# A different order of jobs on TensorE and of steps on VectorE in a fused attention and feed-forward kernel

## What is computed

```
xn = _layernorm(x)
q, k, v = split(xn @ Wqkv + bqkv)
qp, kp = elu(q) + 1, elu(k) + 1
kv = einsum('bsd,bse->bde', kp, v)                 # one sum over the 2048 rows of a batch
attn = (qp @ kv) / (qp @ sum(kp) + 1e-6)
z = layer_norm(xn + attn, g1, b1)
ffn = (silu(z @ Wg + bg) * (z @ Wu + bu)) @ Wd + bd     # Wg and Wu have 682 columns
s = layer_norm(z + ffn, g2, b2)
out = x + s * silu(xn @ (ternary(weight) * scale).T)
```

## Time and profile before

| what | value |
|---|---|
| median of 3 runs | 1211.54 us (1210.9 to 1212.32) |
| the profiled execution | 1212.66 us |
| its span in the profile | 1211.0 us |
| busy: TensorE matmul | 1190.9 us, 98% |
| busy: VectorE | 1082.2 us, 89% |
| busy: ScalarE | 953.3 us, 79% |
| busy: GpSimd | 841.7 us, 70% |

### The profile page before, as it was taken

The page is one execution under the profiler, slowest core; times in us unless marked ns, Lnnn a source line. Parts: engine busy times, 40 slices in busy tenths (PEclk is TensorE's granted clock), DMA queues, the critical chain, the costliest instruction groups (busy, mean ns, idle before and its releaser), DMA issues.

```text
span 1211.0 us, 24021 instructions
## 1 busy us (share of the span) xinstructions
PE 1190.9 (98%) x7550; PEld 1070.2 (88%) x7550; DVE 1082.2 (89%) x2467; ACT 953.3 (79%) x1557; POOL 841.7 (70%) x994
## 2 busy tenths in 40 slices
PE   8999999999999999999999999999999999999997
PEld 6889998989988999989999988999988899888886
DVE  6988999999999999999999999999999999777765
ACT  7787888878888887888878888778797788867753
POOL 3443787767787776787767777667776677766676
PEclk9999999999999999999999999999999999999999
DMA  7213432334432334432234432234332343222201
GB/s 217 74 50 88 123 106 70 88 105 123 123 104 72 87 106 123 118 103 78 87 106 122 121 104 74 74 120 123 108 96 63 101 123 105 70 71 61 76 22 35
DMA packets 137524, 115.61 MB, mean 95 GB/s; under 512 B 12340, under 2 KB 122294, under 8 KB 137399
## 3 DMA queue, kind: packets, MB, share of 16 engines
q1 hardware_dynamic: 137398, 114.08, 32.2%
HBM read 67.38 MB, written 46.67 MB: 94 GB/s over the span
## 4 chain that ended last, share of the span: by engine, by line
PE 86%; DVE 7%; issue 2%; ACT 2%; DMA 1%; POOL 1%; SPq 0%; DVEq 0%; POOLq 0%; ACTq 0%
PE bank L1271 61%; PE d_bank L1271 17%; PE xk_bank L1271 7%; DVE st L922 1%; DMA z_turned<-xa 1%; DMA xa<-z_turned 1%; DVE rz L1054 1%; PE bank L1285 1%; DVE bank L1095 0%; DVE h_l L1105 0%; ACT rz L695 0%; DVE zT_l L1085 0%; POOL norm L569 0%; ACT hs L695 0%; DVE kp L1014 0%
## 5 line engine op out<-in xcount | busy, mean ns | idle before, releaser
L1271 PE MATMUL bank<-zT_h,wgu_h 128*128 128x512 f32 x704 | 275.6, 391 | 1.1 <-DVE rz L1054 1.0
L1271 PE MATMUL bank<-zT_l,wgu_h 128*128 128x512 f32 x704 | 275.7, 392 | 0.0
L1271 PE MATMUL bank<-zT_h,wgu_l 128*128 128x512 f32 x704 | 275.4, 391 | 0.0
L695 ACT ACTIVATE rz<-rz,norm 128x256 f32<-128x256 f32 x252 | 140.5, 596 | 57.7 <-DVE norm L1131 57.1
L569 POOL TENSOR_TENSOR norm<-ve,consts 128x4 f32<-128x4 f32 x64 | 72.9, 1139 | 153.6 <-DVE ve L933 153.5
L1271 PE MATMUL d_bank<-wd_h,h_h 128*128 128x256 f32 x640 | 179.2, 280 | 0.1
L1271 PE MATMUL d_bank<-wd_h,h_l 128*128 128x256 f32 x640 | 179.0, 280 | 0.0
L1271 PE MATMUL d_bank<-wd_l,h_h 128*128 128x256 f32 x640 | 179.0, 280 | 0.0
L1095 DVE SCALAR_TENSOR_TENSOR bank<-bank,hb,hs 128x512 f32<-128x512 f32 x160 | 117.9, 754 | 54.0 <-ACT hs L695 42.3
L695 ACT ACTIVATE h_h<-bank 128x512 fp32r<-128x512 f32 x160 | 95.8, 599 | 80.9 <-DVE bank L1095 80.5
L1271 PEld LDWEIGHTS bank<-zT_l,wgu_h 128*128 128x128 f32 x704 | 132.1, 188 | 28.8
(11 more groups left out here) (163 smaller groups left out, 3576.3 us busy)
## 6 DMA issues: line engine op xcount, KB each, us to landing
xq<-in_L_attn_x_dram SPq DMA_DIRECT2D x32, 512.0 KB, 6.0
xa<-in_L_attn_x_dram SPq DMA_DIRECT2D x31, 512.0 KB, 3.9
out_dram<-rz SPq DMA_DIRECT2D x31, 512.0 KB, 5.0
z_turned<-xa SPq DMA_DIRECT2D x120, 128.0 KB, 3.3
xa<-z_turned SPq DMA_DIRECT2D x30, 512.0 KB, 4.1
turned<-xa SPq DMA_DIRECT2D x108, 128.0 KB, 2.5
xa<-turned SPq DMA_DIRECT2D x27, 512.0 KB, 3.9
rz<-in_L_attn_Wg_dram SPq DMA_DIRECT2D x1, 640.0 KB, 5.2
```

The lines of the kernel that those rows point to most:

```text
L695: return eng.activation(out_, in_, func, **kw).then_inc(S[name], 1)
L1271: ins = eng.matmul(dst, left, right, start=first and n == 0, stop=last and n == len(pairs) - 1, **kw)
```

## The change

Three things move. On TensorE, D 4 goes ahead of K 0, and XK 1 and XK 2 go ahead of U 4 (XK 0 stood there already, and XK 3 stays between U 4 and the last gate-up job). On VectorE, `zT_low` 1 goes ahead of `k_add` 0, `k_low` 1 ahead of `q_elu` 1 and `q_low` 0, and `h_low` 4 ahead of `x_low` 1. And the aggregation that ended `a_stats` becomes a step of its own, `a_aggregate`, which in the steady list stands behind `h_low` 1. No instruction is added or removed, and ScalarE, GpSimd and SyncE keep their order.

```diff
 TENSOR_JOBS = steps("""
-    K 0, D 4, KV 0, KV 1, D 5, K 1, N 0, N 1, N 2, N 3, G 0, U 0, G 1, U 1, G 2, B 0, U 2, Q 0, Q 1,
-    B 1, G 3, D 0, D 1, U 3, G 4, XK 0, U 4, XK 1, XK 2, XK 3, GU 5, D 2, TZ 0, TZ 1, D 3""")
+    D 4, K 0, KV 0, KV 1, D 5, K 1, N 0, N 1, N 2, N 3, G 0, U 0, G 1, U 1, G 2, B 0, U 2, Q 0, Q 1,
+    B 1, G 3, D 0, D 1, U 3, G 4, XK 0, XK 1, XK 2, U 4, XK 3, GU 5, D 2, TZ 0, TZ 1, D 3""")
...
 VECTOR_STEPS = steps("""
-    xk_low 0, zT_low 0, k_add 0, zT_low 1, kv_bias 0, kv_bias 1, kv_low 0, kv_low 1, ffn_rows 0,
+    xk_low 0, zT_low 0, zT_low 1, k_add 0, kv_bias 0, kv_bias 1, kv_low 0, kv_low 1, ffn_rows 0,
...
-    h_low 0, h_rows 1, a_stats 0, h_low 1, q_aggregate 0, h_rows 2, a_norm 0, x_turn 0, attn_norm 0,
...
+    h_low 0, h_rows 1, a_stats 0, h_low 1, a_aggregate 0, q_aggregate 0, h_rows 2, a_norm 0, x_turn 0, attn_norm 0,
...
@@ -956,7 +956,6 @@
                 for t in range(TILES):
                     stats(0, g, t, xa[:, g % 2, t, :])
-                aggregate(0, g)
```

More of the change, by code:

```diff
@@ L99 @@
 VECTOR_STEPS = steps("""
-    xk_low 0, zT_low 0, k_add 0, zT_low 1, kv_bias 0, kv_bias 1, kv_low 0, kv_low 1, ffn_rows 0,
+    xk_low 0, zT_low 0, zT_low 1, k_add 0, kv_bias 0, kv_bias 1, kv_low 0, kv_low 1, ffn_rows 0,
     ffn_rows 1, k_add 1, last_stats 0, attn 0, last_shift 0, attn 1, attn 2, attn 3, h_rows 0, k_max 0,
-    h_low 0, h_rows 1, a_stats 0, h_low 1, q_aggregate 0, h_rows 2, a_norm 0, x_turn 0, attn_norm 0,
-    k_max 1, h_low 2, k_low 0, q_elu 0, z_turn 0, q_elu 1, q_low 0, k_low 1, h_rows 3, h_rows 4,
-    q_low 1, h_low 3, x_low 0, h_rows 5, x_low 1, h_low 4, h_low 5""")
+    h_low 0, h_rows 1, a_stats 0, h_low 1, a_aggregate 0, q_aggregate 0, h_rows 2, a_norm 0, x_turn 0, attn_norm 0,
+    k_max 1, h_low 2, k_low 0, q_elu 0, z_turn 0, k_low 1, q_elu 1, q_low 0, h_rows 3, h_rows 4,
+    q_low 1, h_low 3, x_low 0, h_rows 5, h_low 4, x_low 1, h_low 5""")
 GPSIMD_STEPS = steps("""
@@ L145 @@
 FILL_VECTOR = fill("""
-    a_stats 0 0, a_stats 0 1, a_norm 0 0, a_norm 0 1, setup_k_low 0 0, xT_low 0 0, a_stats 1 0,
+    a_stats 0 0, a_stats 0 1, a_norm 0 0, a_norm 0 1, setup_k_low 0 0, xT_low 0 0, a_stats 1 0, a_aggregate 1 0,
     a_norm 1 0, setup_bk 0 0, xT_low 0 1, k_add 0 0, setup_q_low 0 0, xT_low 1 0, k_add 0 1, k_max 0 0,
-    a_stats 2 0, setup_bq 0 0, k_max 0 1, k_add 1 0, a_norm 2 0, xT_low 1 1, q_elu 0 0, k_max 1 0,
-    q_low 0 0, k_add 1 1, setup_gu_low_0 0 0, xT_low 2 0, k_max 1 1, a_stats 3 0, k_add 2 0, xT_low 2 1,
-    a_norm 3 0, setup_gu_low_1 0 0, q_elu 0 1, k_max 2 0, xT_low 3 0, k_add 2 1, a_stats 4 0, k_max 2 1,
+    a_stats 2 0, a_aggregate 2 0, setup_bq 0 0, k_max 0 1, k_add 1 0, a_norm 2 0, xT_low 1 1, q_elu 0 0, k_max 1 0,
+    q_low 0 0, k_add 1 1, setup_gu_low_0 0 0, xT_low 2 0, k_max 1 1, a_stats 3 0, a_aggregate 3 0, k_add 2 0, xT_low 2 1,
+    a_norm 3 0, setup_gu_low_1 0 0, q_elu 0 1, k_max 2 0, xT_low 3 0, k_add 2 1, a_stats 4 0, a_aggregate 4 0, k_max 2 1,
     setup_v_low 0 0, k_add 3 0, q_low 0 1, xT_low 3 1, a_norm 4 0, setup_d_bias 0 0, k_max 3 0,
-    k_add 3 1, a_stats 5 0, k_max 3 1, xT_low 4 0, setup_ternary 0 0, q_elu 1 0, xk_low 0 0, xT_low 4 1,
+    k_add 3 1, a_stats 5 0, a_aggregate 5 0, k_max 3 1, xT_low 4 0, setup_ternary 0 0, q_elu 1 0, xk_low 0 0, xT_low 4 1,
     k_add 4 0, kv_bias 0 0, kv_bias 0 1, a_norm 5 0, kv_low 0 0, kv_low 0 1, x_turn 5 0, k_max 4 0,
@@ L1260, in _ @@
                     "h_rows": (f, h_rows), "attn": (q, attn), "h_low": (f, h_low), "a_norm": (a + 1, a_norm), "x_turn": (a + 1, x_turn), "x_low": (a + 1, x_low),
-                    "q_aggregate": (q, lambda g, _: aggregate(1, g)), "last_stats": (last, last_stats),
+                    "a_aggregate": (a + 1, lambda g, _: aggregate(0, g)), "q_aggregate": (q, lambda g, _: aggregate(1, g)), "last_stats": (last, last_stats),
                     "attn_norm": (q, attn_norm), "z_turn": (q, z_turn), "last_shift": (last, last_shift),
```

## The result

The changed kernel takes 1228.34 us (median of 4 runs, 1228.14 to 1228.53) where the kernel before takes 1211.81 us beside it (4 runs, 1210.9 to 1212.32). The ratio is 1.0138 (95% interval 1.0123 to 1.0152): 16.5 us slower, past the upper end of the range. The profiled execution has a span of 1226.4 us, 15.4 more than before.

What follows compares the result with a forecast made beforehand. TensorE, 98% busy, was taken as the bound, so only waits counted: -1.8 + 4.8 + 2.0 = +5.0 us on the profiled 1212.66, or 1217.7, giving a median of 1216.5 us. The 8-in-10 range was 1209.5 to 1221.5 us.

Steps and rivals of the forecast that it cites:

- What bounds the kernel: TensorE, busy 98% of the span, sets the time; no matmul goes, so only its waits can be won or lost.
- A late handover costs x + 0.11 us: A TensorE job that waits x loses another 0.11 us, as its first weight load was not done ahead.
- Part one: Aggregation behind `h_low` 1: the 13 waits at Q 1 go, 0.14 us each, a gain of 1.8 us.
- Part two: `zT_low` 1 ahead of `k_add` 0 stands for GpSimd's `xn_low`; VectorE is 0.60 us later, costing 4.8 us at U 0.
- U 0's term: U 0 waits for the late `attn` 0 in 20 iterations, 0.24 us each: 4.8 us, bounds 2.8 to 6.6.
- What is late next: VectorE's remaining 0.36 us delay meets G 4 after `q_elu` 0: 0.1 us in 20 iterations, 2.0 us, bounds 0 to 9.4.
- Part three: XK 1 and XK 2 ahead of U 4, `k_low` 1 ahead of `q_elu` 1: room stays near 0.8 us, cost nothing.
- the third: VectorE's whole 0.60 us returns as waits at U 0, then G 4, XK 2 or U 4: 1225.7 us, chance 0.10.
- The first rival: VectorE keeps the port, does both `zT_low` in a row, GpSimd's `xn_low` behind them: 1209.0 us, chance 0.13.
- The second rival: `xn_low` may get the port first, so the delay stays under U 0's room: 1209.7 us, chance 0.15.
- the forecast's own range: 1212.5 us (2.8 at U 0, nothing at G 4) to 1222 (6.6 at U 0, half the bound at G 4).
- the signs named: `zT_low` 1 about 1.8 us, U 0's matmuls 0.34 apart, 20 more `rz` waits, Q 1's gone, iterations 36.0 to 36.2 us.

Runs made afterwards that it cites:

- f1: p1 with the shift step of `a_norm` moved behind `x_turn`: 1.0035 of the kernel before.
- p1: Kernel before with only the aggregation moved behind `h_low` 1: 1.0065 of the kernel before, +7.9 us.
- u2_aggregate: Changed kernel with the aggregation put back ahead of `h_low` 1: 1.0083 of the kernel before.
- e1: Kernel before with D 0 put ahead of Q 1 on TensorE, VectorE untouched: 0.9995 of the kernel before.
- p2_ztlow: Kernel before with only `zT_low` 1 moved ahead of `k_add` 0: 1.0079 of the kernel before, +9.2 us.
- m1_xnlow: Changed kernel with GpSimd's first `xn_low` moved behind the power `last_rstd`: 1.0176 of the kernel before, 1232.9 us.
- u3_both: Changed kernel with `k_add` 0 back between the two `zT_low` and the aggregation back ahead of `h_low` 1: 1.0003 of the kernel before.
- p3_xk: Kernel before with only XK 1 and XK 2 ahead of U 4, `k_low` 1 ahead of `q_elu` 1 and `q_low` 0: 1.0021, +2.6 us.
- p4_d4: Kernel before with only D 4 ahead of K 0 and `h_low` 4 ahead of `x_low` 1: 1.0014, +1.7 us.

## Why the prediction was wrong

**What bounds the kernel.** Right for the kernel before, and read too narrowly. I took TensorE's waits for the only thing to watch, and the engines around it for something with room. The chain after has 21% of TensorE and 79% of the rest: a delay of VectorE that is larger than the room of a handover isn't caught up there, but is met again further on. Which way around the engines holds the time is not shown. The way through SyncE's transfers and ScalarE's `zT_high` is one, but in f1 `zT_high` was on time and VectorE as late as in p1.

**A late handover costs x + 0.11 us.** Right: 0.06 us from release to start and 0.34 us to the second matmul, at U 0 as in the earlier trace rows.

**Part one, "the gain is 13 x 0.14 = 1.8 us".** The wrong step, and the larger error: +7.9 us was measured alone. That is 9.7 us of the 11.5 by which the forecast of +5.0 fell short of +16.5. The waits at Q 1 did go. What failed is the sentence "VectorE may meet as a wait of up to 0.1 us ahead of `a_norm`; nothing of TensorE hangs on it directly". There was no wait to speak of, yet `a_norm` took 0.42 us more where GpSimd's next step had started 0.06 us ahead of it; behind `a_norm` hang `x_turn`, SyncE's queue, `z_turned` and `zT_high`. GpSimd's steps came 0.5 us later against VectorE, `q_low` 1 stood 0.44 us longer, and TensorE did wait: for `x_low` 1 ahead of K 0, 4.4 us in 18 places for 0.7 in 3, and in the changed kernel at U 3 and D 4, where u2_aggregate has no waits. That the moved aggregation costs this is shown by p1 and u2; through which of these steps is argued. Whether even the gain of 1.8 us is real stays open: with the same waits removed, e1 is no faster.

**Part two, the port.** The mechanism was right: `zT_low` 1 stands behind `zT_low` 0 for `xn_low`, in 16 of the 20 iterations here and in 19 in p2_ztlow, and U 0 waits in all 20. The Trainium skill's page "SBUF — State Buffer", section "Who interferes with whom", says that issue order decides who blocks, and the trace agrees: `zT_low` 1 takes 1.78 us where `xn_low` has got in ahead of it, and 0.68 in m1_xnlow, where `xn_low` comes later. The size was off. U 0's term, 20 x 0.24 = 4.8 us, came out at 10.2 in the changed kernel and 6.6 in p2_ztlow, since the delay was 0.73 us in iteration 14 in place of 0.60 (0.60 for `k_add`, and 0.13 since the pair itself starts later) and 0.82 as the median of the 20, 0.63 in p2. With a room of 0.5 us each tenth over it costs 2 us in 20 iterations. I had named 6.6 as the upper bound. The rest of the 10.2 us is hardly from part one, as u2_aggregate, without it, has 9.3 us at U 0; it came with the moves on TensorE and the VectorE steps that go with them, by what way was not looked into.

**What is late next, "G 4 ... 2.0 us".** The size was near for p2, the place wrong: G 4 does not wait. In p2 the delay is met at Q 1 and Q 0, 5.2 us where it was 2.5. In the changed kernel Q 1 is covered, and U 3 waits with 7.0 us, which neither part brings about alone. I had followed one rest of a delay along VectorE's list, and had not gone back over each job with the new phases.

**Part three, "cost nothing".** Right for the pieces together: u3_both, 1.0003. Each piece alone on the kernel before costs 1.7 to 2.6 us, about as much as can be told. Together with part two they are not free of effect, as the 9.3 us at U 0 for 6.6 show, though the time is nearly the same (1.0083 and 1.0079).

**The rivals.** The result is nearest to the third, "the delay spreads", 1225.7 us with a chance of 0.10: its price was near, and its reason against ("VectorE's idle time late in each iteration") did not hold, as D 4's waits show. But it had part one with the wrong sign, too, and named G 4, XK 2 or U 4 as the places, so the near price is partly luck. The first rival is excluded: `xn_low` starts ahead of `zT_low` 1. The second rival's case, `xn_low` with the port first, did come in four of the 20 iterations, but U 0 waited there all the same. No rival had the aggregation as a loss. (The end of the forecast's own range was added up as 1222 us; its terms give 1221.0.) In the signs named: `zT_low` 1 standing, the 0.34 us at U 0 and the 20 added waits for `rz` came (28 for 9); iterations 12 to 14 took 36.22, 36.82 and 36.66 us where 36.0 to 36.2 was forecast, and that was the first sign of a second cause.

**What stays open.** How the moved aggregation costs its time is known in part: no run removes `a_norm`'s stretch, or that of `q_low` 1, with the rest in place, and why VectorE is 0.4 us late from the start of each iteration in p1 and f1 alike was not found. Why p3_xk and p4_d4 each cost a little alone and nothing together was not followed up.

## What to carry to other kernels

In a hand-ordered kernel where VectorE and GpSimd both run above two thirds, a step that moves by half a microsecond changes who has the port at each later meeting, so list these meetings over a whole iteration, with the room of each, before calling a shift free. Follow a late result through in-order queues too, not only through the engine that does it. And do not book a removed wait as a gain before it is measured: here the edit that removed 1.8 us of waits without touching VectorE was no faster.

## What was not expected of the hardware

- An instruction of 128x4 elements stands for the port like a large one: `last_shift` took 1.22 us instead of 0.14 beside `xn_low`, in all 26 iterations of m1_xnlow.
- A step that is released by GpSimd (`a_norm`, by the power) can take longer beside the next GpSimd instruction, which starts just ahead of it: 1.79 to 1.81 us for 1.38 as the median in every kernel of the table with the moved aggregation, whether a product or a power stood behind. That it stands for the port is read from the order of the starts; no run has it without a GpSimd instruction there.
- `a_norm` reads one tile and two columns of statistics; it isn't only the steps with two full tiles in SBUF, which I had looked at, that can be held up beside GpSimd.
- Half a microsecond of shift turns around who stands: `q_low` 1 took 0.72 us when it began 0.57 us behind the start of `last_add` 3 and 0.12 us ahead of `sum_k` 2, and 1.16 us when it began 0.12 us behind the start of `last_add` 3.
